# Graph aggregation in 256 PSUM columns, with the self-loop as a scaled row on ScalarE

## The reference

```python
# cut: the graph layer; x is (2048, 256), adj is (2048, 2048) of zeros and ones
deg = max((adj != 0).sum(-1), 1)
xn = layernorm(x)
dinv = rsqrt(deg)[:, None]
a_norm = dinv * (adj + eye) * dinv      # both factors scale the rows
pooled = a_norm @ xn + xn
x = x + relu(pooled @ W + b)
# then x = x + experts(layernorm(x)) + gelu(layernorm(x) @ sw1.T) @ sw2.T
```

## Time and profile before

| What | us |
|---|---|
| Runs of the kernel before | 511.6, 511.74, 513.07 |
| Median | 511.74 |
| The profiled execution: span, first to last instruction | 512.6 |
| Quarter 0 ends (first matmul of `agg_end`) | 53.36 |
| The same for quarters 1, 2 and 3 | 89.78, 142.52, 195.42 |
| PE busy | 461.1 (90%) |
| POOL busy | 323.0 (63%) |
| DVE busy | 263.1 (51%) |
| ACT busy | 198.3 (39%) |

### The profile page before, as it was taken

One profiled execution on the slowest core, in us unless ns is written; L12 is line 12 of the kernel. 1 busy time (PEld: TensorE's weight loads), 2 busy tenths in 40 slices (PEclk: granted clock), 3 DMA queues, 4 the chain that ended last, 5 costly groups with the idle time before them and its releaser, 6 DMA issues.

```text
span 512.6 us, 8736 instructions
## 1 busy us (share of the span) xinstructions
PE 461.1 (90%) x2632; PEld 395.9 (77%) x2633; DVE 263.1 (51%) x484; ACT 198.3 (39%) x430; POOL 323.0 (63%) x296
## 2 busy tenths in 40 slices
PE   6889987999999989998387999699999999999992
PEld 5778766987789878898275888588878888888871
DVE  5997798617681668497143334223342333333330
ACT  3556631663456344654132223222232232232230
POOL 3999894387738783557547266758565847888111
PEclk9999988999999999999589999989999999999997
DMA  8564141923150341765378777787868787465100
GB/s 253 189 221 150 41 164 30 305 70 123 42 165 1 99 148 27 244 223 181 128 195 271 263 256 263 243 270 260 282 211 297 243 275 232 62 75 73 12 1 0
DMA packets 45497, 84.44 MB, mean 165 GB/s; under 512 B 7712, under 2 KB 21152, under 8 KB 43424
## 3 DMA queue, kind: packets, MB, share of 16 engines
q1 hardware_dynamic: 24640, 44.05, 28.0%
q0 software_dynamic: 7536, 29.39, 18.4%
q10 hardware_dynamic: 13296, 10.67, 7.1%
HBM read 74.74 MB, written 10.26 MB: 166 GB/s over the span
## 4 chain that ended last, share of the span: by engine, by line
PE 50%; POOL 13%; DMA 9%; issue 8%; DVE 3%; ACT 2%; another core or an unknown queue 2%; POOLq 1%; ACTq 0%; SPq 0%
PE bank L1155 20%; POOL a_lo L348 8%; PE bank L1081 7%; PE bank L1180 6%; PE bank L1100 5%; DMA eraw<-in_experts 5%; POOL ering L395 4%; PE bank L1181 3%; DMA ering<-in_experts 3%; PE bank L1102 3%; PE bank L1166 2%; PE bank L995 2%; POOL gel_lo L364 1%; DVE rows L673 1%
## 5 line engine op out<-in xcount | busy, mean ns | idle before, releaser
L395 POOL TENSOR_TENSOR ering<-eraw,ering 128x512 fp32r<-128x512 f32 x84 | 105.8, 1290 | 61.3 <-DMA ering<-in_experts 35.1
L1155 PE MATMUL bank<-ering,xsT_hi 128*128 x368 | 124.4, 410 | 9.3 <-POOL ering L395 9.2
L348 POOL TENSOR_TENSOR a_lo<-araw,a_hi 128x512 fp32r<-128x512 f32 x64 | 96.1, 1520 | 27.7 <-ACT a_hi L475 27.4
L995 PE MATMUL bank<-zz,a_hi 128*128 128x512 f32 (+1 forms) x256 | 94.7, 409 | 4.5 <-POOL a_lo L348 4.4
L1155 PEld LDWEIGHTS bank<-ering,xsT_hi 128*128 128x128 f32 x368 | 71.2, 193 | 26.7 <-issue 10.5
L909 DVE SCALAR_TENSOR_TENSOR hid<-bank,row_wt,sil 128x512 f32<-128x512 f32 x46 | 34.5, 751 | 105.5 <-ACT sil L592 105.5
L1155 PE MATMUL bank<-ering,xsT_lo 128*128 x184 | 74.1, 403 | 0.0
L997 PE MATMUL bank<-zz,a_lo 128*128 128x256 f32 (+1 forms) x256 | 72.9, 285 | 0.0
L592 ACT ACTIVATE sil<-bank 128x512 f32<-128x512 f32 x46 | 27.5, 598 | 112.4 <-PE bank L1155 108.0
L364 POOL TENSOR_TENSOR gel_lo<-gel,gel_hi 128x256 fp32r<-128x256 f32 x52 | 39.8, 765 | 46.8 <-ACT gel_hi L528 45.7
L1180 PE MATMUL bank<-ering,hidT_hi 128*128 x184 | 67.4, 405 | 1.2 <-DVE hidT_lo L917 1.2
(11 more groups left out here) (143 smaller groups left out, 800.3 us busy)
## 6 DMA issues: line engine op xcount, KB each, us to landing
eraw<-in_experts SPq DMA_DIRECT2D x96, 256.0 KB
araw<-in_adj_t SPq DMA_DIRECT2D x32, 512.0 KB, 5.1
ering<-in_experts POOLq DMA_DIRECT2D x8, 1536.0 KB, 8.7
ering<-in_experts POOLq DMA_DIRECT2D x8, 1024.0 KB, 7.0
ering<-in_experts POOLq DMA_DIRECT2D x8, 512.0 KB, 5.7
sorted_x<-zeros ACTq DMA_DIRECT2D x1, 2967.0 KB, 16.7
xs<-sorted_x ACTq DMA_DIRECT2D x23, 128.0 KB
resid<-in_x SPq DMA_DIRECT2D x4, 512.0 KB, 9.0
```

The costliest lines, as they stand in the source:

```text
L348: pool.tensor_tensor(a_lo[:, u % AR, :], araw[:, u // CJ, u % CJ, :], a_hi[:, u % AR, :].bitcast(F32), ALU.subtract).then_inc(adj_lo_ok, 1)
L395: pool.tensor_tensor(ering[:, slot, 1, c * ECW:(c + 1) * ECW], eraw[:, c % ER, :], ering[:, slot, 0, c * ECW:(c + 1) * ECW].bitcast(F32), ...
L995: pe.matmul(acc(it)[:, :], a_hi[:, s, it * P:(it + 1) * P], zt, start=first, stop=False)
L1155: ins = pe.matmul(bank[2 * w + h][:, :], a[:, k, :], ering[:, bass.ds(slot, 1), part, at:at + BANK].rearrange("p a n -> p (a n)"), start=n ...
```

## The change

- **agg_part**: the matmul with 512 columns becomes two with 256 columns. Both go to columns 0 to 255 of the bank, as the third one already did. The last of the 16 steps closes the sum.
- **agg_end** and **copy_sums** go, with their semaphores. So does DVE's add of the two halves (L750).
- **inverse_degree** makes a third small value, `dinv1 = 1/deg + 1`, and raises `dinv_ok` only behind it.
- **self_loops** is new on ACT, in the place of `copy_sums`: it waits for `dinv_ok` and scales the four copies of z by `dinv1` in place.
- **add_bias** is new on POOL: the bias adds of a quarter's four tiles, each behind its scaled row. In quarter 0 the adds leave the loop of `first_lows` and stand behind all 16 `a_lo`.
- **finish_gnn** does `acc * dinv2 + norm` from PSUM in one instruction for each tile, behind the bias add, and only this frees the bank.
- **degrees(q)** stands ahead of `gate(q-1)` on PE, and `inverse_degree(q)` ahead of `logits(q-1)` on DVE, in quarters 1 to 3.

```diff
@@ POOL
             def first_lows():
-                pool.wait_ge(bias_loaded, 16)
                 for t in range(NT):
                     adj_low(t % (RAW * CJ), t)
-                    pool.wait_ge(z_copied, t + 1)
+            def add_bias(q):
+                pool.wait_ge(bias_loaded, 16)
+                for it in range(QT):
+                    t = q * QT + it
+                    pool.wait_ge(self_loop, t + 1)
                     pool.tensor_tensor(norm[:, t, :], norm[:, t, :], bias[:], ALU.add).then_inc(bias_added, 1)
...
             first_lows()
+            add_bias(0)
             adj_lows(1, 0, AR)
             for q in range(1, NQ):
                 adj_lows(q, AR, NT)
+                add_bias(q)
@@ ACT
-            def copy_sums(q):
-                act.wait_ge(agg_sum, q + 1)
-                for it in range(QT):
-                    act.activation(agg[:, it, :], acc(it)[:, 0:D], ACT.Copy).then_inc(agg_copied, 1)
+            def self_loops(q):
+                act.wait_ge(z_copied, NT)
+                act.wait_ge(dinv_ok, q + 1)
+                for it in range(QT):
+                    t = q * QT + it
+                    act.activation(norm[:, t, :], norm[:, t, :], ACT.Copy, scale=dinv1[:, it:it + 1]
+                                   ).then_inc(self_loop, 1)
@@ DVE
-                dve.reciprocal(dinv2[:], deg[:]).then_inc(dinv_ok, 1)
+                chained(dve.reciprocal(dinv2[:], deg[:]))
+                settle()
+                dve.tensor_scalar(dinv1[:], dinv2[:], 1.0, None, ALU.add).then_inc(dinv_ok, 1)
             def finish_gnn(q):
-                for it in range(QT):
-                    dve.wait_ge(agg_copied, q * QT + it + 1)
-                    dve.tensor_tensor(agg[:, it, :], acc(it)[:, D:2 * D], agg[:, it, :], ALU.add
-                                      ).then_inc(agg_free, 1)
+                dve.wait_ge(agg_tile, (q + 1) * NT)
+                for it, t in enumerate(group(q)):
+                    dve.wait_ge(bias_added, q * QT + it + 1)
+                    dve.scalar_tensor_tensor(agg[:, it, :], acc(it)[:, 0:D], dinv2[:, it:it + 1],
+                                             norm[:, t, :], ALU.mult, ALU.add).then_inc(agg_free, 1)
                 dve.wait_ge(agg_free, (q + 1) * QT)
-                dve.wait_ge(dinv_ok, q + 1)
-                dve.wait_ge(bias_added, (q + 1) * QT)
-                for it, t in enumerate(group(q)):
-                    chained(dve.scalar_tensor_tensor(agg[:, it, :], agg[:, it, :], dinv2[:, it:it + 1],
-                                                     norm[:, t, :], ALU.mult, ALU.add))
-                settle()
...
-                logits(q - 1)
                 inverse_degree(q)
+                logits(q - 1)
@@ PE
-                    pe.matmul(acc(it)[:, :], a_hi[:, s, it * P:(it + 1) * P], zt,
+                    pe.matmul(acc(it)[:, 0:D], a_hi[:, s, it * P:(it + 1) * P], zt[:, 0:D],
                               start=first, stop=False)
+                    pe.matmul(acc(it)[:, 0:D], a_hi[:, s, it * P:(it + 1) * P], zt[:, D:2 * D],
+                              start=False, stop=False)
                     ins = pe.matmul(acc(it)[:, 0:D], a_lo[:, s, it * P:(it + 1) * P], zt[:, 0:D],
-                                    start=False, stop=False)
+                                    start=False, stop=last)
-            def agg_end(q):
-                for it in range(QT):
-                    ins = pe.matmul(acc(it)[:, :], ident_r[:], zz[:, q * QT + it, :, :].rearrange("p h d -> p (h d)"),
-                                    start=False, stop=True)
-                ins.then_inc(agg_sum, 1)
...
                 pe.wait_ge(split_lo, 4)
+                pe.wait_ge(xfT_lo_ok, 2 * q)
+                degrees(q)
                 gate(q - 1)
-                degrees(q)
```

More of the change, by code:

```diff
@@ L107, in gnn_moe @@
     dinv2 = place("dinv2", [P, QT], F32)
+    dinv1 = place("dinv1", [P, QT], F32)
     logit = place("logit", [P, NT, E], F32)
@@ L217, in gnn_moe @@
         agg_tile = sem("agg_tile")
-        agg_sum = sem("agg_sum")
+        self_loop = sem("self_loop")
         deg_ps = sem("deg_ps")
         dinv_ok = sem("dinv_ok")
-        agg_copied = sem("agg_copied")
         agg_free = sem("agg_free")
@@ L547, in split_shared @@
                 act.activation(sw2_r[:, :, 0, :], sw2_raw[:], ACT.Copy).then_inc(split_hi, 1)
+            def self_loops(q):
[5 more added lines that the diff above has]
+                                   ).then_inc(self_loop, 1)
             adj_highs(1, 0, AR)
-            copy_sums(0)
+            self_loops(0)
             for q in range(1, NQ):
@@ L558, in _ @@
                 adj_highs(q, TURN + AR - 1, NT)
-                copy_sums(q)
+                self_loops(q)
                 load_table(ACT.Gelu)
@@ L807, in _ @@
                 count_chunks(q, RAW, NC)
+                inverse_degree(q)
                 logits(q - 1)
-                inverse_degree(q)
                 finish_gnn(q)
@@ L983, in z_tile, with agg_part @@
                 ins.then_inc(z_ps, 1)
-            def agg_part(j, s, n, first=False):
+            def agg_part(j, s, n, first=False, last=False):
                 pe.wait_ge(adj_lo_ok, n + 1)
@@ L1029, in _ @@
                 pe.wait_ge(z_ok, t + 1)
-                agg_part(t, t % AR, t)
-            pe.wait_ge(z_copied, NT)
-            agg_end(0)
+                agg_part(t, t % AR, t, False, t == NT - 1)
             degrees(0)
@@ L1042, in agg_quarter @@
                 for j in range(TURN, NT):
-                    agg_part(j, j % AR, q * NT + j)
-                agg_end(q)
+                    agg_part(j, j % AR, q * NT + j, False, j == NT - 1)
             def xf_transposes(q):
```

## The result

| What | before | after |
|---|---|---|
| Median of four runs, us | 511.87 | 522.91 |
| Lowest and highest, us | 511.6, 513.07 | 520.84, 530.86 |
| Profiled execution: time, span | span 512.6 | 520.84, 518.9 |
| PE busy, us | 461.1 | 457.7 |
| DVE busy, us | 263.1 | 257.1 |

The account below looks back on a forecast made before the run. The prediction took DVE, in exchange with POOL, as the bound, PE waiting. Quarter 1's +2.1 and the ends' +0.95, +2.0, +1.9 sum to 6.95, span 512.6 to 519.6, as a median 518.7 us; range 513.5 to 523.

Follow-up runs that it names:

- both moves: Kernel after with the table load ahead of the scaled rows and POOL's first four subtractions of quarter 1 ahead of quarter 0's bias adds; one run, 517.55 us.

## What to carry to other kernels

Work that comes off a busy engine is worth nothing if the new form of it needs a value that is ready last: ask of each new operand when its maker is done, and read that from the timeline before counting instructions. A wait in front of a queue costs what the queue could have done ahead: here POOL's four subtractions ran in the shadow of quarter 0, and one line's place was worth 3.3 us. Two engines that shut each other out of SBUF are to be scheduled into each other's pauses; eight instructions took 3.1 us in a pause and 5.3 outside one.

## What the runs showed of the hardware

- DVE with two operands in SBUF stops for POOL's instruction, and the price grows with POOL's queue: the same four adds to `resid` took 1.43 in a POOL pause, 2.53 before, 3.28 in one version and 5.2 in the kernel after, beside an unbroken row of `a_lo`. With one of the two in PSUM four instructions took 1.66 beside `a_lo`. The Trainium skill's page "SBUF — State Buffer", section "SBUF: two separate sides", describes the ports that the two share as an exclusive lock that is held for a whole instruction; the rows agree.
- ACT's scaled row of 256 columns steps by 0.40 with a factor per partition and by 0.31 with a constant.
- A pause of PE of 2.08 us, with work at full clock on both sides, was followed by 3.4 us at 1.2 GHz behind quarter 3, but not behind quarters 1 and 2 with the same pause. In the other versions with these pauses it came behind quarter 1 alone (table load first), behind 2 and 3 (subtractions first), behind 1 and 2 (constant scale) and behind none (both moves); with the pause filled by routing matmuls it came behind all three. What decides stays open. The long pauses were plain: each of the seven traces with 4.1 to 5.3 us ahead of quarter 1 has PE at 1.2 GHz for 3.4 to 6.8 us around its end and behind it, none of the six with 0.9 to 1.1 has.
- The same expert part took 246.3 to 251.4 us in different executions, as many as 5 us from a part that no edit touched. Marks ahead of it tell edits apart that whole spans do not. But a mark can be moved by a stretch of the clock too: the one of the earlier trace rows is in one of thirteen traces, and it put 1.3 us into the comparisons of three versions with before.
